# The last MLP is begun ahead of the last attention tile's end, GpSimd makes the low parts of its weights, and its layers are reordered

## The reference, cut to what matters

```python
x = x + attention1(layer_norm(x), ctx)      # 16 heads of 128
x = x + attention2(layer_norm(x), ctx)
h = layer_norm(x) * scale + offset
x = x + gelu(h @ w_fc1 + b_fc1) @ w_fc2 + b_fc2     # 256 -> 1024 -> 256
```

## Time and profile before

| | |
|---|---|
| median of 3 runs | 1130.79 us |
| the profiled execution's own time | 1130.49 us |
| its span, first to last instruction | 1128.4 us |
| busy: TensorE, weight load, VectorE, ScalarE, GpSimd | 92%, 72%, 59%, 46%, 36% |
| mean granted TensorE clock | 0.980 |
| last tile's steps, from the end of the steady steps | about 975 to 1024 us |
| last MLP, from its first matmul to its end | 1024.0 to 1128.4 us |

### The profile page before, as it was taken

How to read it: one execution, slowest core, us unless ns; L and a number is a source line. 1 busy time by engine, 2 the same in 40 slices (tenths; PEclk the granted TensorE clock), 3 DMA queues, 4 the chain that set the end, 5 groups by cost and what they waited for, 6 DMA issues and landing times.

```text
span 1128.4 us, 17672 instructions
## 1 busy us (share of the span) xinstructions
PE 1033.0 (92%) x7036; PEld 810.7 (72%) x7036; DVE 663.2 (59%) x1127; ACT 519.1 (46%) x1036; POOL 402.6 (36%) x416
## 2 busy tenths in 40 slices
PE   6999889887789799989999999999999999978997
PEld 3666555555566699887787777777777777648997
DVE  3657888778568669722444545775444454574552
ACT  2556777676566454433333332333323333324543
POOL 2534578688966523200222112331122211222230
PEclk9999999998999999999999999999999999999999
DMA  9000000000000060010000013310000000100000
GB/s 307 36 2 1 1 1 1 1 1 1 1 1 1 24 220 1 1 53 23 1 1 1 1 49 102 112 38 1 1 1 1 1 1 7 69 1 1 29 19 29
DMA packets 17046, 32.26 MB, mean 29 GB/s; under 512 B 3522, under 2 KB 8388, under 8 KB 16452
## 3 DMA queue, kind: packets, MB, share of 16 engines
q1 hardware_dynamic: 16964, 31.13, 8.1%
HBM read 29.03 MB, written 2.10 MB: 28 GB/s over the span
## 4 chain that ended last, share of the span: by engine, by line
PE 74%; ACT 8%; POOL 7%; issue 5%; DVE 5%; DMA 0%; POOLq 0%; DVEq 0%; ACTq 0%
PE work L775 10%; PE work L891 10%; PE scores L830 9%; PE work L847 5%; PE work L880 4%; PE work L561 3%; PE work L631 3%; PE work L632 3%; PE work L633 3%; PE scores L631 3%; PE scores L633 3%; PE scores L632 2%; PE work L518 2%; PE work L862 2%; PE work L436 2%
## 5 line engine op out<-in xcount | busy, mean ns | idle before, releaser
L891 PE MATMUL work<-pair,probsT 128*128 128x256 f32 x512 | 120.3, 388 | 11.0 <-ACT pair L1777 8.8
L1857 POOL TENSOR_SCALAR stat<-stat 128x2 f32<-128x2 f32 (+1 forms) x49 | 11.1, 227 | 315.4 <-DVE stat L1008 313.9
L891 PEld LDWEIGHTS work<-pair,probsT 128*128 128x128 f32 x512 | 95.7, 192 | 35.3 <-issue 20.3
L775 PE MATMUL work<-ctxT,w 128*128 128x128 f32 x1008 | 118.2, 275 | 2.7 <-ACT pair L1777 1.1
L775 PEld LDWEIGHTS work<-ctxT,w 128*128 128x128 f32 x1008 | 116.3, 192 | 4.1 <-issue 2.0
L830 PE MATMUL scores<-pair,act_bufs 128*128 128x512 f32 x256 | 115.2, 592 | 0.0
L1768 ACT ACTIVATE pair<-work 128x512 f32<-128x512 f32 x64 | 38.2, 598 | 154.5 <-PE work L847 154.5
L1758 ACT ACTIVATE kvT<-work,cols 128x128 f32<-128x128 f32 x124 | 35.5, 369 | 153.2 <-PE work L775 153.2
L2005 POOL TENSOR_TENSOR probs<-probs,smax 128x1024 f32<-128x1024 f32 x22 | 42.0, 1907 | 157.6 <-DVE smax L1398 157.6
L1378 DVE TENSOR_REDUCE smax<-scores 128x16 f32<-128x1024 f32 x32 | 39.2, 1225 | 77.2 <-PE scores L830 77.2
L830 PEld LDWEIGHTS scores<-pair,act_bufs 128*128 128x128 f32 x256 | 46.3, 190 | 46.0 <-issue 45.9
(11 more groups left out here) (194 smaller groups left out, 2634.0 us busy)
## 6 DMA issues: line engine op xcount, KB each, us to landing
w<-in_l_wk SPq DMA_DIRECT2D x8, 512.0 KB, 6.1
w<-in_l_wq SPq DMA_DIRECT2D x8, 512.0 KB, 6.7
w<-in_l_wo SPq DMA_DIRECT2D x8, 512.0 KB, 7.5
w<-in_l_wv SPq DMA_DIRECT2D x8, 512.0 KB, 5.4
out<-x SPq DMA_DIRECT2D x8, 256.0 KB, 2.2
x<-in_x SPq DMA_DIRECT2D x1, 1536.0 KB, 9.3
pair<-in_l_fc SPq DMA_DIRECT2D x1, 1024.0 KB, 7.1
pair<-in_l_pr SPq DMA_DIRECT2D x1, 1024.0 KB, 9.1
```

The source lines that it names most:

```text
L775: last = mm(bank[:, h * P:(h + 1) * P], w[:, c, (4 * g + h) * K3:(4 * g + h + 1) * K3], ctxT[:, c, p * P:(p + 1) * P], start=(c == 0), sto ...
L891: last = mm(step_banks(j + 1)[0][:, 0:D], probsT_bufs[j % 2][:, q, :], pv[n % 2][:, bb, q, :], start=(q == 0), stop=(q == GH // 2 - 1))
```

## The change

**Weights.** The eight low parts of weight quarters are subtracted on GpSimd (semaphore p_wl) and not on VectorE, in the same steps 28 to 31, behind GpSimd's other work of the step.

**Norms.** Items 0 and 1 are normed for the MLP in steps 28 and 29, not 30 and 31.

**Start.** The first item's transposes stand at the end of step 30; its affine, high and low parts in steps 30 and 31; its four last_hidden and the second item's transposes at the start of step 32, ahead of tile 31's transposes and output. In step 31 the transposes of tile 30 wait for that affine, as they write the bank which it reads. last_hidden(0, f) waits for tile 30's subtraction (f = 0, 1) or tile 31's (f = 2, 3), where each waited for tile 31's.

**Order of the MLP.** For items 1 to 7 TensorE runs hidden 0, hidden 1, the next item's transposes, hidden 2, the projection of the item before, hidden 3. Before it was hidden 0, 1, projection, transposes, hidden 2, 3. The other engines' orders follow.

```diff
@@ tensor: tile_transposed
                         first_free(j + 1)
+                        if j + 1 == 4 * B - 1:
+                            e.wait_ge(d_mT, 2 * B + 2)
@@ tensor: last_source(b)
                 if b >= 2:
                     e.wait_ge(d_mT, 2 * (B + b - 2) + 2)
-                else:
-                    e.wait_ge(d_lT, 2 * B)
-                    e.wait_ge(a_lpT, 8 * B)
-                    e.wait_ge(a_pv, 16 * PAIRS)
-                    e.wait_ge(d_lr, 4 * B - 1)
+                    e.wait_ge(d_lr, 4 * B - 1)
+                elif b == 0:
+                    third_free(4 * B - 2)
+                else:
+                    e.wait_ge(a_lpT, 8 * B - 2)
@@ tensor: last_hidden(b, f)
-                e.wait_ge(d_wl, 8 + 4)
+                e.wait_ge(p_wl, 4)
-                    e.wait_ge(d_lsub, 4 * B)
+                    e.wait_ge(d_lsub, 4 * B - 1 + f // 2)
@@ tensor: steps
+                if j == 4 * B:
+                    for f in range(4):
+                        last_hidden(0, f)
+                    last_source(1)
                 if tile_of(j - 1) is not None:
                     tile_transposed(j - 1)
...
+                if j == 4 * B - 2:
+                    last_source(0)
@@ tensor: the last MLP
-            last_source(0)
-            for b in range(B + 1):
-                for f in range(2):
-                    if b < B:
-                        last_hidden(b, f)
-                if b > 0:
-                    last_projected(b - 1)
-                if b + 1 < B:
-                    last_source(b + 1)
-                for f in range(2, 4):
-                    if b < B:
-                        last_hidden(b, f)
+            for b in range(1, B):
+                last_hidden(b, 0)
+                last_hidden(b, 1)
+                if b + 1 < B:
+                    last_source(b + 1)
+                last_hidden(b, 2)
+                last_projected(b - 1)
+                last_hidden(b, 3)
+            last_projected(B - 1)
@@ vector: steps
-                if j >= 4 * B - 4 and j < 4 * B:
-                    for q in range(2):
-                        weight_low((j - 28) // 2, 2 * (j % 2) + q)
-                if j in (4 * B - 2, 4 * B - 1):
-                    last_norm(j - 4 * B + 2)
+                if j in (4 * B - 4, 4 * B - 3):
+                    last_norm(j - 4 * B + 4)
+                if j == 4 * B - 2:
+                    last_affine(0)
+                    last_low(0)
@@ vector: the last MLP
+            for b in range(B):
+                hidden_low(b, 0)
+                if b + 1 < B:
+                    last_affine(b + 1)
+                hidden_low(b, 1)
+                if b + 1 < B:
+                    last_low(b + 1)
+                hidden_low(b, 2)
+                if b + 2 < B:
+                    last_norm(b + 2)
+                if b > 0:
+                    mlp_residual(B + b - 1)
+                hidden_low(b, 3)
+            mlp_residual(2 * B - 1)
@@ scalar: steps
+                if j == 4 * B - 1:
+                    source_high(0)
+                if j == 4 * B:
+                    last_hidden(0, 0)
+                    last_hidden(0, 1)
                 if tile_of(j - 1) is not None:
                     tile_out(j - 1)
@@ scalar: the last MLP
+                for f in range(3):
+                    if b > 0 or f == 2:
+                        last_hidden(b, f)
+                    if f == (2 if b == 0 else 1) and b + 1 < B:
+                        source_high(b + 1)
+                last_hidden(b, 3)
@@ gpsimd: steps
+            def weight_low(w, q):
+                both = w1_parts if w == 0 else w2_parts
+                n = raw.shape[2] // 4
+                e.wait_ge(a_wh, 8 + 4 * w + q + 1)
+                g.tensor_tensor(flat(both[1])[:, q * n:(q + 1) * n], raw[:, w, q * n:(q + 1) * n],
+                                flat(both[0])[:, q * n:(q + 1) * n].bitcast(F32), ALU.subtract).then_inc(p_wl, 1)
...
-                if j in (4 * B - 2, 4 * B - 1):
-                    rstd(("m3", j - 4 * B + 2), TT)
+                if j in (4 * B - 4, 4 * B - 3):
+                    rstd(("m3", j - 4 * B + 4), TT)
+                if 4 * B - 4 <= j < 4 * B:
+                    for q in range(2):
+                        weight_low((j - 28) // 2, 2 * (j % 2) + q)
```

More of the change, by code:

```diff
@@ L907, in value_constants, with last_source, last_hidden, last_projected @@
                 mm(step_banks(j)[1][:, 0:D], ones[:, :], value_sum, start=True, stop=True).then_inc(pe_bias, 1)
+            def last_source(b):
+                bank = work[2 + b % 2]
+                e.wait_ge(*NORMS["m3", b])
+                if b >= 2:
+                    e.wait_ge(d_mT, 2 * (B + b - 2) + 2)
+                    e.wait_ge(d_lr, 4 * B - 1)
[3 more added lines that the diff above has]
+                    e.wait_ge(a_lpT, 8 * B - 2)
+                transposes(bank, fixed[2 + b % 2]).then_inc(pe_mx, 1)
+            def last_hidden(b, f):
+                e.wait_ge(a_sh, B + b + 1)
+                e.wait_ge(d_sl, B + b + 1)
+                e.wait_ge(a_wh, 8 + 4)
+                e.wait_ge(p_wl, 4)
+                if b > 0:
+                    e.wait_ge(a_g, 4 * (B + b - 1) + f + 1)
+                else:
+                    e.wait_ge(d_lsub, 4 * B - 1 + f // 2)
+                for j in range(2):
+                    for c in range(DC):
+                        last = products(fbank[f][:, j * T:(j + 1) * T],
+                                        [w[:, c, (2 * f + j) * P:(2 * f + j + 1) * P] for w in w1_parts],
+                                        [v[:, c, :] for v in src_parts[b % 2]], c == 0, c == DC - 1)
+                last.then_inc(pe_f1, 1)
+            def last_projected(b):
+                e.wait_ge(a_hh, 4 * (B + b) + 4)
+                e.wait_ge(d_hl, 4 * (B + b) + 4)
+                e.wait_ge(a_wh, 16)
+                e.wait_ge(p_wl, 8)
+                if b < 2:
+                    e.wait_ge(a_lpT, 8 * B)
+                    e.wait_ge(a_pv, 16 * PAIRS)
+                    e.wait_ge(d_lr, 4 * B)
+                else:
+                    e.wait_ge(d_mr, B + b - 1)
+                for t in range(TT):
+                    for f in range(FC):
+                        last = products(work[b % 2][:, t * D:(t + 1) * D],
+                                        [v[:, f, t * P:(t + 1) * P] for v in hid_parts[b % 2]],
+                                        [w[:, f, :] for w in w2_parts], f == 0, f == FC - 1)
+                last.then_inc(pe_f2, 1)
             for j in STEPS:
@@ L945, in last_hidden @@
[L945 to L948, removed]
-                e.wait_ge(d_wl, 8 + 4)
-                if b > 0:
-                    e.wait_ge(a_g, 4 * (B + b - 1) + f + 1)
-                else:
-                    e.wait_ge(d_lsub, 4 * B)
[L954 to L966, removed]
-                    e.wait_ge(a_lpT, 8 * B)
-                    e.wait_ge(a_pv, 16 * PAIRS)
-                    e.wait_ge(d_lr, 4 * B)
-                else:
-                    e.wait_ge(d_mr, B + b - 1)
-                for t in range(TT):
-                    for f in range(FC):
-                        last = products(work[b % 2][:, t * D:(t + 1) * D],
-                                        [v[:, f, t * P:(t + 1) * P] for v in hid_parts[b % 2]],
-                                        [w[:, f, :] for w in w2_parts], f == 0, f == FC - 1)
-                last.then_inc(pe_f2, 1)
@@ L1420, in last_norm, with last_affine, last_low, hidden_low @@
                 ln_finish(("m3", b), xb(b), fixed[2 + b % 2], TT)
[L1422 to L1427, removed]
+            def last_affine(b):
+                e.wait_ge(pe_mx, B + b + 1)
+                if b < 2:
+                    e.wait_ge(pe_ls, 2 * (2 * B - 2 + b) + 2)
+                else:
+                    e.wait_ge(a_sh, B + b - 1)
+                affine(work[2 + b % 2], fixed[b % 2], "l3_gm", "l3_bm", d_mT)
+            def last_low(b):
+                e.wait_ge(a_sh, B + b + 1)
+                e.wait_ge(d_mT, 2 * (B + b) + 2)
+                v.tensor_tensor(src_parts[b % 2][1], fixed[b % 2], src_parts[b % 2][0].bitcast(F32),
+                                ALU.subtract).then_inc(d_sl, 1)
+            def hidden_low(b, f):
+                e.wait_ge(a_hh, 4 * (B + b) + f + 1)
+                hi, lo = (p[:, 2 * f:2 * f + 2, :] for p in hid_parts[b % 2])
+                v.tensor_tensor(lo, hid_whole[f], hi.bitcast(F32), ALU.subtract).then_inc(d_hl, 1)
             for j in STEPS:
@@ L1798, in weight_high @@
                 act(flat(both[0])[:, q * n:(q + 1) * n], raw[:, w, q * n:(q + 1) * n], ACT.Copy).then_inc(a_wh, 1)
[L1800 to L1813, removed]
             def source_high(b):
@@ L1839, in last_hidden @@
                 act(hid_parts[b % 2][0][:, 2 * f:2 * f + 2, :], hid_whole[f], ACT.Copy).then_inc(a_hh, 1)
-            source_high(0)
-            for b in range(B):
-                for f in range(2):
```

(24 more changed lines are left out.)

34 lines of the change are left out of this document (2 added, 32 removed).

## The result

The changed kernel takes 1125.03 us (median of 4 runs, 1124.04 to 1125.96), the kernel before 1131.15 in the same session: ratio 0.9949, 95% interval 0.9931 to 0.9966. Two later sessions gave 1124.59 against 1131.89 and 1124.98 against 1131.29; medians leave out two disturbed executions of the first of them, 1501 us of the changed kernel and 3602 us of the kernel before. So it is 6.1 to 7.3 us faster; 1123.7 was forecast. The profiled execution took 1125.96 us, its span is 1123.8.

What follows compares the result with a forecast made beforehand. TensorE, 92% busy, bounds the kernel; time lies only in its standstills and half clock. 8.8 gained less 1.8 for clock makes 7.0 us off 1130.49: 1123.5, with 0.3 for the median 1123.7 us; range 1121.3 to 1127.3.

Steps and rivals of the forecast that it cites:

- The measure: From hidden(1, 0) on both kernels have the same matmuls left, so its start, 1031.76 before, measures the gain.
- the new start: Step 32: four hidden groups (5.7 us) and item 1's transposes (0.44) run ahead of tile 31's transposes, output ending at 1019.4.
- The new gap: Ahead of hidden(1, 0): 3.6 us of addition, hidden_low, affine, high and low; start at 1023.0, 8.8 us gained.
- the held norms: Steps 28 and 29: GpSimd subtractions hold VectorE's norms; tile 29's maximum +0.3 us, tile 30's about 1.0 late, covered by 0.7.
- 1.7, end 980.5: Step 28: item 0's norm pair takes 1.7 us, its first half waiting out GpSimd's subtraction, and ends at 980.5.
- the stated bound of 1.3: Step 28: upper bound of +1.3 us on tile 29's maximum if both norm halves are held and the bias is late.
- nothing is lost there: Step 28: the value bias ends at 981.2 and TensorE needs it at 981.69, so no loss.
- On VectorE their removal is what frees tile 31: Steps 28 to 31: taking the eight weight subtractions off VectorE frees tile 31's chain; no separate size given.
- The half clock: Behind the new 3.6 us gap TensorE falls to half clock, giving back 1.8 us; bounds 0 and 1.8 + 1.8.
- a second low spell and held norms: Rival: tile 29's gap of 2.6 also costs 1.8, VectorE held up to 1.3 more: 1125.5 to 1127 us; chance 0.18.
- The order of the MLP: Last MLP, new order: no stall, source has 8.6 us where it had 2.9; at the end the same 2.36 idle.

Runs made afterwards that it cites:

- e8: Kernel before with only the start of the change (norms, item 0's source, hidden groups, item 1's transposes moved); weights and MLP order as before: 1126.65 us against 1131.29.
- e4: Kernel before the change with only the new order of the last MLP on all engines: 1131.26 us against 1131.53, ratio 0.9996.
- e5: Kernel before the change with only the eight weight subtractions moved to GpSimd: 1131.36 us against 1131.53, ratio 0.9998.
- e3: Changed kernel with two hidden_low, item 1's affine and low part and item 2's norm ahead of tile 31's addition, high part earlier: 1120.36 us, 4.23 below it.
- e2: Changed kernel, but GpSimd waits in steps 28 and 29 for VectorE's norm before its weight subtractions: 1123.36 us, 1.23 below the changed kernel.
- e1: Changed kernel with the eight weight subtractions back on VectorE at the end of steps 28 to 31: 1125.27 us against 1124.59 for the changed kernel.
- e7: Changed kernel with edits of e2 and e3, plus hidden(7, 3) and its low part ahead of item 6's projection and addition: 1113.95 us, 0.9839 of kernel before.

## Why the prediction came out right, and which steps of it did not

**The measure and the new start: right.** The matmuls from hidden(1, 0) on take 93.34 us in both, and the four hidden groups fill the wait of tile 31. TensorE's rows around them, 1008.50 + 3.72 to 1020.00, show no gap but the copy's 0.74. e8 shows that the start alone (norms, item 0's source and hidden groups) gains 4.64 us, while e4 and e5 show no measurable gain for either other part by itself. The norms and the hidden groups were not moved one without the other.

**The new gap: right.** 3.6 us forecast, 3.46 measured in two profiles of the changed kernel, in the chain that was written down (addition, hidden_low, affine, high, low); e3 takes it away and gains 4.23 between the medians, the gap and clock behind it. The clock was low behind this gap in all five profiles that have 3.46 or 4.06.

**Steps 28 and 29, the held norms: mis-sized.** Forecast "1.7, end 980.5", +0.3 on tile 29's maximum; measured 2.63 and +0.94 to tile 28's output (11.59 us after tile 27's addition, for 10.65). The prediction reads from the earlier trace rows that the first half of the pair is held. It was the other: the multiplication, and VectorE's L1014 alone in two windows beside it (columns: us, busy of VectorE, instructions),
```profile
945.97 1.91 POOL L2005 TENSOR_TENSOR probs_late<-probs_late,smax 128x1024 f32<-128x1024 f32 x1 [1.39 <-DVE smax L1398]
```
```profile
945.96:946.30 0.34, 0.34 (x2) 1.00 0.00 0
946.30:947.60 1.30, 1.30 (x1) 1.00 0.00 0
```
The first half began at 945.80, ahead of the multiplication, and took 0.32; the second began at 946.04 and ended at 948.03, just behind it. In the changed kernel each half begins just behind a GpSimd subtraction (980.47 behind 980.41, 981.74 behind 981.63) and takes 1.35. So an operation is held if the other engine's began ahead of it, and here two did. The cost lay within the stated bound of 1.3. The sentence "nothing is lost there" failed as well: TensorE needs the value bias for the second half of tile 28's transposes already (tile_transposed waits for d_vT), hence the 0.68.

In step 29 tile 30's maximum was to be 1.0 late and covered by 0.7. It was 2.5 us late (996.84, where 993.08 of before and the 1.27 by which equal code is later here make 994.35), and not quite covered: from tile 29's output to tile 30's it takes 9.47 us (996.85 to 1006.32) for 8.76 before and 0.44 of new transposes, 0.27 more. Together the holds cost 0.94 + 0.27 = 1.21 us where 0.3 was forecast, and e2, which takes them away, gains 1.22 to hidden(1, 0).

The lock of the Trainium skill (SBUF — State Buffer, "Who interferes with whom") agrees with these runs, down to a 128x16 clamp of 1.23 us for 0.17; e2 takes the overlap away, and the norm is 0.74.

**"On VectorE their removal is what frees tile 31": wrong.** e1 puts them back and is no slower to hidden(1, 0) (50.01 us for 50.18; 0.7 between the medians, within their scatter); e5 moves them alone and gains 0.17. With the subtractions gone, item 0's norm with its round trip over GpSimd keeps tile 31 as late. The change moved that norm to step 28, and this and the new place of the hidden groups carry the gain together; their shares are open. The forecast sum did not rest on the sentence, as it timed tile 31 from its scores, so the total survived it.

**The half clock: a little too dear, and not the only spell.** 1.8 us were given for one spell behind the new gap. It was there in both profiles and cost 1.3 to 1.5: from hidden(1, 0) to the last projection they take 87.32 and 87.20 us, for 85.83 before and 85.93 in e3, which have no spell there. The 1.8 came from 7.5 less a calculated 5.7, but the last projection at full clock takes 6.0. The first profile had a second spell at tile 28's output (5.38 for 3.69) and none at the end, the second profile none at tile 28 and one at the end. The rival "a second low spell and held norms" happened in part: the held norms in both profiles, the spell at tile 28 in one.

**How near the sum came.** It put hidden(1, 0) at 47.74 us after tile 27's addition (1023.0 less 975.26); the second profile has 48.48, the first 50.18 with its spell of 1.7. To the last addition the two gained 6.66 and 6.32 us of the 7.0, so the holds that were priced too low and the spell that was priced too high cancelled in part, which is luck. The median is 1.3 us above the forecast, of which 0.4 lie in the kernel before (1131.15 in the session, for 1130.79); the last step of the sum is also 0.1 short, as 1123.49 and 0.3 make 1123.8.

**The order of the MLP: right.** No gap in items 2 to 7, and none in e4's either but the 1.01 at item 2. The last gap stayed at 2.36 as forecast; e7 shows that it could have been had by moving hidden(7, 3) and its low part ahead of item 6's projection and addition.

**Left open.** Why a low spell follows a gap of 2.3 us in one execution and not in the next was not tried. Nor is the 0.8 to 1.4 us between the medians of e8 and e1 settled beyond the 0.6 of its gap.

## What to carry to other kernels

An operation moved to an idle engine isn't free if the two engines hold each other: look at what the other engine starts at the same moment, and put a wait so that the one on the path goes first. Before crediting the removal of work that stands ahead of a late instruction, ask what else it would have waited for: here two subtractions filled a wait for another engine, and taking them away left the wait. And where an engine idles for 9.70 us ahead of an instruction that waits, everything queued behind it that is ready should go in front.

## What the runs showed of the hardware

Equal code up to step 27 ended at 974.45 to 978.68 us in twelve profiles of kernels that differ only behind it, so one profile tells nothing below 4 us of a total; differences have to be taken from a common instruction near the change. Gaps of 2.28 to 2.36 us on TensorE were followed by half clock in some executions and by full clock in others: behind 2.28 or 2.31 us tile 28's output took 5.38 in four of eleven profiles and 3.69 in the rest, and behind 2.36 us the last projection took 7.5 in six of ten and 6.0 in the rest. Behind 3.46 to 4.06 us the clock was low in five of five. A GpSimd subtraction of 128x512 with fp32r output took 1.25 to 1.32 us, on VectorE 0.69. Which engine waits is set by which operation began first: VectorE's norm half took 0.32 to 0.41 us when it began ahead of GpSimd's operation, and 1.35 to 1.99 when it began just behind.
